# Operand loads of a head in three row groups with a repeating source, and the first rows issued between the loads of attention A

## The reference

```
x = x + attn_a(layernorm(x))
x = x + ffn(layernorm(x))
x = x + attn_b(layernorm(x))
x = x + ffn(layernorm(x))

attn_a:  q, k, v = heads(x @ W + b)          16 heads of width 16, 2048 positions
         pos     = sinusoid(2048) @ Wp + bp  per head
         score   = ((q + u) @ k.T + relative_shift((q + v) @ pos.T)) / 4
         out     = softmax(score) @ v,  then @ Wo + bo
attn_b:  causal attention, 16 heads, without positions
ffn:     relu(h @ W1 + b1) @ W2 + b2
```

## Time and profile before

| | |
|---|---|
| median of 3 runs | 11704.78 us (11701.66 to 11712.92) |
| the profiled execution | 11740.77 us, of it 11739.0 us span |
| granted TensorE clock, mean | 0.925 |
| busy share: PE, PEld, DVE, ACT, POOL | 82%, 59%, 53%, 57%, 25% |
| moved by DMA | 2482.16 MB in 452690 packets |
| attention A of the first batch | from about 155.8 us to about 1880 us |
| attention B of the last batch | from 10828.5 us |

### The profile page before, as it was taken

One profiled execution on the slowest core, in us unless ns is written; L12 is line 12 of the kernel. 1 busy time (PEld: TensorE's weight loads), 2 busy tenths in 40 slices (PEclk: granted clock), 3 DMA queues, 4 the chain that ended last, 5 costly groups with the idle time before them and its releaser, 6 DMA issues. The chain is left out here.

```text
span 11739.0 us, 268351 instructions
## 1 busy us (share of the span) xinstructions
PE 9666.4 (82%) x95520; PEld 6878.1 (59%) x95520; DVE 6260.3 (53%) x14730; ACT 6698.0 (57%) x11009; POOL 2935.3 (25%) x3520
## 2 busy tenths in 40 slices
PE   5887888899687788899968878889986787888999
PEld 3555556666455556566635555556664555555666
DVE  3555553675355555376445555537744555553764
ACT  3665664675365666366546656637744565663764
POOL 2333332001233333200123333320012333332001
PEclk8999999899799999999979999999998999999999
DMA  6999993100699999210079999920007999992000
GB/s 233 337 337 335 345 342 118 49 23 19 216 356 328 334 355 346 102 27 24 17 242 339 341 335 344 339 96 25 24 26 256 338 332 326 346 345 86 24 24 26
DMA packets 452690, 2482.16 MB, mean 211 GB/s; under 512 B 78976, under 2 KB 100992, under 8 KB 188864
## 3 DMA queue, kind: packets, MB, share of 16 engines
q1 hardware_dynamic: 451264, 2463.71, 62.1%
HBM read 1280.34 MB, written 1183.07 MB: 210 GB/s over the span
## 5 line engine op out<-in xcount | busy, mean ns | idle before, releaser
L658 DVE CUSTOM_DVE_ANT_0 z<-sc,z 128x1024 f32<-128x1024 f32 x2048 | 2497.0, 1220 | 2356.4 <-DMA z<-rel_rows 1959.4
L716 POOL TENSOR_SCALAR z<-z,nmax 128x1024 f32<-128x1024 f32 x2048 | 2271.2, 1120 | 4649.0 <-DVE nmax L668 4649.0
L631 ACT ACTIVATE pT<-rg 128x512 f32<-128x512 f32 x4096 | 2445.2, 598 | 855.0 <-PE rg L541 796.3
L639 ACT ACTIVATE rel<-rg 128x512 f32<-128x512 f32 x3072 | 1727.0, 596 | 1895.0 <-PE rg L522 1886.7
L522 PE MATMUL rg<-pos_s,qv_s 96*128 96x512 bf16 x4096 | 1646.3, 410 | 1382.2 <-DVE rel L693 1261.7
L541 PE MATMUL rg<-ident,z 128*128 128x128 f32 x16384 | 2597.7, 283 | 87.6 <-issue 78.6
L541 PEld LDWEIGHTS rg<-ident,z 128*128 128x128 f32 x16384 | 2067.8, 146 | 827.4 <-ACT rel L639 259.9
L522 PEld LDWEIGHTS rg<-pos_s,qv_s 96*128 96x128 bf16 x4096 | 487.6, 120 | 1872.7 <-DVE rel L693 1505.8
L1006 DVE CUSTOM_DVE_ANT_0 z<-sc,mask 128x1024 f32<-128x1024 f32 (+7 forms) x1536 | 1359.3, 910 | 229.2 <-PE sc L825 176.0
L945 ACT ACTIVATE pT<-rg 128x512 f32<-128x512 f32 (+3 forms) x1792 | 928.3, 550 | 776.2 <-PE rg L878 763.3
L953 ACT ACTIVATE z<-z,nmax 128x128 f32<-128x128 f32 (+15 forms) x1024 | 1226.7, 1198 | 90.0 <-POOL nmax L971 78.2
(11 more groups left out here) (93 smaller groups left out, 8191.7 us busy)
## 6 DMA issues: line engine op xcount, KB each, us to landing
rel_rows<-rel SPq DMA_DIRECT2D x1024, 1024.0 KB, 11.3
z<-rel_rows SPq DMA_DIRECT2D x1024, 1024.0 KB, 9.1
xnT<-qu_parts SPq DMA_DIRECT2D x792, 64.0 KB, 2.3
xnT<-v_heads SPq DMA_DIRECT2D x132, 256.0 KB, 4.2
v_heads<-rel SPq DMA_DIRECT2D x8, 4096.0 KB, 12.5
k_sb<-k_parts SPq DMA_DIRECT2D x408, 64.0 KB, 2.3
qv_s<-qv_parts SPq DMA_DIRECT2D x384, 64.0 KB, 9.5
pos_s<-pos_parts SPq DMA_DIRECT2D x384, 64.0 KB, 10.4
```

The costliest lines, as they stand in the source:

```text
L631: e.activation(pT[:, t % 2, q * CH:(q + 1) * CH], rg[:, T_BANK[q], :], ACT.Exp, scale=SCALE).then_inc(p_ready[q], 1)
L639: e.activation(rel[:, r % RING, c * CH:(c + 1) * CH], rg[:, R_BANK[c], :], ACT.Copy).then_inc(r_copied[c], 1)
L658: e.tensor_tensor_reduce(out=zs, in0=scf[:, 2 * half * CH:2 * (half + 1) * CH], in1=zs, scale=1.0, scalar=-3.0e38, op0=ALU.add, op1=ALU.ma ...
L716: e.tensor_scalar(zs, zs, 1.0, nmax[:, n % 2:n % 2 + 1], ALU.mult, ALU.add).then_inc(AA[done], 1)
```

## The change

All operand loads go by three groups in place of six slots, and the tile's rows are dealt out anew. Group 0 is the even rows 0 to 94 (48 rows): the three query parts against key part 0. Group 1 is the odd rows 1 to 63 (32 rows): query parts 0 and 1 against key part 1. Group 2 is the odd rows 65 to 95 (16 rows): query part 0 against key part 2. The six products are the same. A group takes two transfers. The query's reads its 3, 2 or 1 parts with one access pattern of three dimensions (16 rows, parts, 4 KB). The key's reads its one part 3, 2 or 1 times with a step of 0. A head takes 6 + 6 + 1 = 13 transfers, of the same 384 rows of 4 KB plus v.

In the steady part of attention A the groups go out at the steps 1 to 3 of a head (q+u and k), v at 4, and q+v and pos at 8 to 10. In the run-in only the q+v and pos groups of head 0 come ahead of the steps; the groups of q+u and k of head 0, its v, and the q+v and pos groups of head 1 follow one per step, each behind the rows written in that step.

```diff
-QPART = [0, 1, 2, 0, 1, 0]
-KPART = [0, 0, 0, 1, 1, 2]
+GROUP = [(0, KROWS, 3), (1, 64, 2), (65, KROWS, 1)]
...
-        QK_INC = 16 * 2 * len(QPART)
+        QK_INC = 16 * 2 * len(GROUP)
...
-        def load_part(e, dst, src, h, a, part, done):
-
-            e.dma_start(dst[a::SLOTS, :],
-                        src[bass.ds(h, 1), part * HD:(part + 1) * HD, :].rearrange("a r s -> (a r) s")).then_inc(done, 16)
-
-        def load_pair(e, q, k, q_src, k_src, h, slots, done):
-
-            for a in slots:
-                load_part(e, q, q_src, h, a, QPART[a], done)
-                load_part(e, k, k_src, h, a, KPART[a], done)
+        def load_group(e, q, k, q_src, k_src, h, i, done):
+
+            first, last, reps = GROUP[i]
+            rows = slice(first, last, 2)
+            e.dma_start(q[rows, :], q_src[bass.ds(h, 1), 0:reps * HD, :].rearrange("a (r d) s -> (a d) r s", d=HD)
+                        ).then_inc(done, 16)
+            e.dma_start(k[rows, :], k_src[bass.ds(h, 1), i * HD:(i + 1) * HD, :]
+                        .rearrange("a (r d) s -> (a d) r s", d=HD).to_broadcast([HD, reps, S])).then_inc(done, 16)
+
+        def load_pair(e, q, k, q_src, k_src, h, done):
+
+            for i in range(len(GROUP)):
+                load_group(e, q, k, q_src, k_src, h, i, done)
...
-            every = range(SLOTS)
-            load_pair(e, qv_s[0], pos_s[0], qv_d, pos_d, 0, every, qv_loaded[0])
-            load_pair(e, qu_s[0], k_s[0], qu_d, k_d, 0, every, AA["qk_loaded0"])
-            load_v(e, 0, 0, AA["v_loaded0"])
-            load_pair(e, qv_s[1], pos_s[1], qv_d, pos_d, 1, every, qv_loaded[1])
+            load_pair(e, qv_s[0], pos_s[0], qv_d, pos_d, 0, qv_loaded[0])
+
+            def first_heads(s):
+
+                i = s + R_LEAD
+                if i < 3:
+                    load_group(e, qu_s[0], k_s[0], qu_d, k_d, 0, i, AA["qk_loaded0"])
+                elif i == 3:
+                    load_v(e, 0, 0, AA["v_loaded0"])
+                elif i < 7:
+                    load_group(e, qv_s[1], pos_s[1], qv_d, pos_d, 1, i - 4, qv_loaded[1])
...
-                if at in range(1, 7) and not (final and hd + 1 >= HB):
+                if at in range(1, 4) and not (final and hd + 1 >= HB):
...
-                    load_pair(e, qu_s[nxt], k_s[nxt], qu_d, k_d, e.snap(p * HB + (hd + 1)), (at - 1,),
-                              AA[f"qk_loaded{nxt}"])
-                if at == 7 and not (final and hd + 1 >= HB):
+                    load_group(e, qu_s[nxt], k_s[nxt], qu_d, k_d, e.snap(p * HB + (hd + 1)), at - 1,
+                               AA[f"qk_loaded{nxt}"])
+                if at == 4 and not (final and hd + 1 >= HB):
...
-                if at in range(8, 14) and not (final and hd + 2 >= HB):
+                if at in range(8, 11) and not (final and hd + 2 >= HB):
...
                 if s >= 0:
                     next_heads(p, base, s, final)
+                else:
+                    first_heads(s)
...
             def load_qk(h, hd):
-                load_pair(e, qu_s[hd], k_s[hd], qu_d, k_d, h, range(SLOTS), BB[f"qk_loaded{hd}"])
+                load_pair(e, qu_s[hd], k_s[hd], qu_d, k_d, h, BB[f"qk_loaded{hd}"])
```

More of the change, by code:

```diff
@@ L784, in next_heads @@
                         settle(e)
-                    load_pair(e, qv_s[hd % NB], pos_s[hd % NB], qv_d, pos_d, e.snap(p * HB + (hd + 2)), (at - 8,),
-                              qv_loaded[hd % NB])
+                    load_group(e, qv_s[hd % NB], pos_s[hd % NB], qv_d, pos_d, e.snap(p * HB + (hd + 2)), at - 8,
+                               qv_loaded[hd % NB])
             def step(p, base, s, here):
```

## The result

The median of 12 runs is 11749.83 us (11722.41 to 11808.36), against 11695.14 us (11652.05 to 11715.59) of the kernel before, whose 12 runs here include the three shown earlier. The ratio is 1.0051, with a 95% interval from 1.0034 to 1.0067: 55 us slower, where 51 us faster was forecast. The profiled execution has a span of 11766.6 us, 27.6 us more than that of before.

The account below looks back on a forecast made before the run. It took attention A to be bound by transfers. Four batches of 9.0 us (first rows) plus 3.8 us (start of attention B) gave 51.2 us off, from 11704.8 to 11653.6 us, with a range of 11600 to 11692.

Parts of the forecast that it names:

- What bounds the kernel: Attention A is bound by transfers: queue share 1.00 at 339 GB/s from 200 to 1800 us, PE busy 1283 of 1600.
- First operands of attention A: Start of attention A: six issues at 0.635 us in place of twelve, PE starts at 161.2, 3.8 us earlier.
- rival (3): Operand loads: a group's issue takes as long as what it replaces, about 1.3 us; 21 us gained, 11684; chance 0.08.
- (5): Load patterns: they don't spread over all 16 queues; 278 us lost, 11932; chance 0.03.
- the 1 us that I had named as a sign: Operand loads: the forecast is wrong if a group's issue is over 1 us long.
- First rows: Attention A's run-in: first write at 165.0, 14.4 us earlier, less 5.4 for moved bytes, net 9.0 us per batch.
- Rival (4): Attention A: the ramp pays back all its head start, only attention B's 15 us stay, 11690; chance 0.08.
- Start of attention B: Six issues in place of twelve: PE starts 5.3 us after the first issue, not 9.1; 3.8 us gained per batch.
- The body: Steady part of attention A: 12 transfers fewer per head, same rows; the number of transfers put at nothing.
- the 0.5 us that I had named as a sign: Body: the forecast is wrong if its heads become longer or shorter by more than 0.5 us.
- Rival (2): Body: lumps delay the next read by 0.77 us per set, 89 us lost against 51 gained, 11743; chance 0.09.
- Rival (1): Body: the number of transfers has a price, fewer save 1.0 us per head, 58 us more, 11595; chance 0.07.

Follow-up runs that it names:

- spread kernels: The changed kernel with one group transfer a step in attention A's body in place of two, and variants of it; the first measured 11543.97 us, ratio 0.9945.
- the cut kernels: The changed kernel and its version with one group transfer a step, 21 of 29 load sets per batch cut to 512 of 2048 columns: ratios 0.9926 and 0.9890.
- the slots in lumps: The kernel before, its old 16-row transfers issued 3, 2 and 1 slots a step in attention A's body: 11837.44 us, ratio 1.0212.
- the spread kernel with big and small in turn: The kernel of one group transfer a step, with row order 48, 16, 48, 16, 32, 32 in place of 48, 48, 32, 32, 16, 16: 11514.89 us, ratio 0.9938.
- spread, lead 9: The changed kernel with one group transfer a step, R_LEAD left at 9, rerun beside the longer-lead kernels: 11427.92 us, ratio 0.9947 to the kernel before.
- spread, lead 10: The kernel of one group transfer a step with R_LEAD 10 in place of 9: 11059.32 us, ratio 0.9622 to the kernel before.

## Why the prediction was wrong, point by point

**What bounds the kernel: half wrong.** I read the share of 1.00 at 339 GB/s as a stage bound by transfers, whose bytes cost 1/339 us per KB wherever they lie. The queues were indeed never empty. But 339 was no ceiling: the same queues gave 374 GB/s, still at 1.00, once a read no longer waited for a write issued two steps before (spread kernels on one chip, 353 with lead 9). DVE's 820 waits for landed rows fit both readings. The wait that told them apart was SP's own for the landing of `rel_rows` writes. It is not among my rows, and I looked at it only as one wait among several. It was the largest of SP's waits in the kernel before:

```profile
SPq L233 <- DMA rel_rows<-rel: 2376.5, 903, 6.7
```

This reading was wrong, but it is not shown to be what cost the forecast: with the wait gone, a lump was as dear as before.

**First operands of attention A: right.** PE started at 161.33, forecast 161.2; the six issues came at 0.66 us, forecast 0.635. The transfers of 48 rows issue nearly like those of 16, so rival (3) is out, and so is (5): the body moved 335 GB/s. Behind the first write, with the queues filling, three key-side issues took 1.38 to 1.55 us, over the 1 us that I had named as a sign; the second and third write still went out 2.69 and 2.85 us behind the one before.

**First rows: right in the sum.** The first write went out at 165.05, forecast 165.0. At the read of tile 16 the lead over before was 9.1 us on the first chip and 8.9 on the second, forecast 9.0. Rival (4), which had it used up, is out. What I named as its cause was half right only: with 19 transfers first the read of tile 16 comes as early, so the gain is that of fewer issues. I had not seen that 19 issues end at 168 us by themselves.

**Start of attention B: right in kind, a little less.** From the first issue to PE it took 9.13 us before and takes 6.19 in batch 4 (5.6 in the three others), forecast 5.3. In batch 4 the last load lands 2.88 us after its issue, where 2.13 was in my sum. The stage as a whole gains 2.7 us per batch (10.8 over all four, from SP's meetings), forecast 3.8.

**The body: the step that failed.** I put it at nothing and wrote that queues which never run dry lose nothing by the order. They lost 18.5 us per batch on the first chip and 21.7 on the second. Of the 29 sets of a batch 27.7 lie in the body, so that is 0.67 and 0.78 us for each. A head of the body grew by 1.4 us on both chips, past the 0.5 us that I had named as a sign. Rival (2) had 0.77 us as its price and 0.44 us as the point from which it decides: on average about the price of a lump's extra bytes was paid, with hardly any of it made good. Its time, 11743, is close to the measured 11749.83, and I gave it 0.09. The sum of the terms closes for the profiled execution: 4 x (18.5 - 9.1) - 10.8 = 27 us, measured 27.6.

The row that could have warned me was there. Twelve old transfers cost 1.95 us where their bytes at 339 GB/s should cost 2.3. I took this as "bytes explain it", with room to spare. It hinted that spread bytes came cheap (1.2 us per MB by the cut kernels), so that bunching them could take that discount away. My sample was also small and high: its two differences average 1.97 us (the last no-load stretch of batch 1 is 38.50 us, and the mean of 1.95 was a slip), but over all heads of the four batches twelve loads cost 1.4 us at the steps 1 to 7 and 1.6 at 8 to 14, and 1.0 and 0.65 in the second chip's profile of the same kernel.

**Rival (1)**, that fewer transfers make the body faster, is not shown: on the second chip the spread kernels' bodies (1516.8 and 1519.6) are 4 to 7 us under that of before (1523.9), within what two profiles differ by.

**What stays open.** That the lump's bytes cost the body time is shown (the cut kernels), and that a lump is dear without the repeated source; with the old transfers (the slots in lumps) it is dear too, but there SP's issues have a part in it. Why the lighter steps don't give the time back is not. The landing loop is excluded as the only reason. A like loop through the four `z` buffers is left (SP's wait for PE's transposes, 290.3 us above). The sums of that wait don't speak for it: from 300 to 1700 us it is 167.7 us in the kernel before on the same chip, but 299.9 in the spread kernel with big and small in turn, which doesn't lose the time. No fifth buffer was tried.

## What to carry to other kernels

Transfers of a stage that runs in step with a ring of buffers are better dealt out in small portions per step than merged into lumps of few steps: here one group transfer a step turned +0.5% into -0.55%. A DMA share of 1.00 said that packets were always in flight, not that the rate was at its ceiling; before taking it as the bound, look at what the issuing engine waits for. If that wait is for the landing of a transfer, try one more step of lead: here one constant was worth 3.0% by itself and 3.8% together with the spread groups, the best version that ran.

## What the runs showed of the hardware that I had not expected

- Full queues have no fixed rate. At a share of 1.00 nearly the same mixture moved 335 (changed), 339 (before), 353 (spread, lead 9) and 374 GB/s (spread, lead 10); in the same stretches the mean 8 KB packet took 380, 377, 362 and 344 ns, while over half of them took 309 ns or less in each. I read this as waiting inside a packet's duration, which the share counts as busy.
- SP's issue time hardly goes by rows: with idle queues 48 rows of 4 KB in the new patterns took 0.60 to 0.70 us, and 32 or 16 rows 0.58 to 0.59; of the old transfers of 16 rows the first of a stage took 0.60 to 0.63 and the others 0.58 to 0.59.
- A transfer of 48 rows on idle queues landed about 0.8 us later than one of 16 (3.0 to 3.2 us in the two starts of batch 1, against 2.1 to 2.3 before), so merging three loads into one saves issues and gives a part back in landing.
- The kernel before differed by 1.7% between the sets of runs (11497.94 to 11695.14 us), more than any edit before the lead was touched, apart from the lumped slots. Two lots on one chip differed by 0.2% (11603.74 and 11580.34).
